# A twelve-layer latent network: keys of the first cross-attention by features, norms in halves, the last layer in one piece

## The reference

```python
def _L0_xattn_ref(x, latents, mask, ...):          # x = ctx_1024, latents = layernorm(x), 16 heads of 64
    xn = layernorm(x, ln_x_g, ln_x_b)
    ln = layernorm(latents, ln_l_g, ln_l_b)
    q = ln @ Wq
    kv = concatenate([xn @ Wkv, ln @ Wkv], axis=1)  # 1601 + 64 keys of each batch
    sim = rmsnorm(q, qn_g) * scale @ rmsnorm(k, kn_g).T
    attn = softmax(where(padded_mask, sim, max_neg))
    return attn @ v @ Wout + bout
...
def _L2_xattn_ref(x1, x2, x3, mask, Wq, Wk, Wv):    # x2 = x3 = ctx_1024, one head of 256
    weights = softmax(q @ k.T / 16 + mask)
    return weights @ v
...
def _L3_ffn_ref(x, W_qkv, b_qkv, W_gate, b_gate, W_experts, b_experts):
    attn_out = softmax(q @ k.T / 4) @ v             # 16 heads of 16, over the 64 latents of a batch
    gate = softmax(x @ W_gate + b_gate)             # 8 experts, the top 2 kept
    expert_out = einsum('bsd,edf->bsef', x, W_experts) + b_experts
    moe_out = einsum('bsef,bse->bsf', expert_out, combine)
    return attn_out + moe_out
...
    x = x + _L0_xattn_ref(ctx_1024, _layernorm(x, axis=-1), ...)   # and eleven more: L0_attn ... L3_ffn
```

## Time and profile before

| | |
|---|---|
| time, median of 3 runs | 3185.78 us (3185.38 to 3188.05) |
| the profiled execution | 3181.54 us, its span 3179.8 us |
| mean granted clock of PE | 0.947 |
| PE busy (matmul) | 2795.1 us, 88% |
| DVE busy | 1643.3 us, 52% |
| ACT busy | 1091.3 us, 34% |
| POOL busy | 522.6 us, 16% |
| L0_xattn | 8.4 to 1254, 1245.6 us |
| L1_xattn, L1_attn, L1_ffn | 504, 295, 223 us |
| L2_xattn, L2_attn, L2_ffn | 137, 95, 167 us |
| L3_xattn, L3_attn, L3_ffn | 234, 53, 117.8 us |

### The profile page before, as it was taken

How to read it: one execution, slowest core, us unless ns; L and a number is a source line. 1 busy time by engine, 2 the same in 40 slices (tenths; PEclk the granted TensorE clock), 3 DMA queues, 4 the chain that set the end, 5 groups by cost and what they waited for, 6 DMA issues and landing times. The chain is left out here.

```text
span 3179.8 us, 43613 instructions
## 1 busy us (share of the span) xinstructions
PE 2795.1 (88%) x17456; PEld 1893.7 (60%) x17456; DVE 1643.3 (52%) x3618; ACT 1091.3 (34%) x1933; POOL 522.6 (16%) x280
## 2 busy tenths in 40 slices
PE   5899999999999998779999978998975689799876
PEld 2466666666666666545656535665962357688644
DVE  5556465655656443545555545763541250177563
ACT  2333333333333332225555436641321252211120
POOL 2112020202112000000000004761010041144200
PEclk8899999999999999889999989998987799899898
DMA  4123223131323211130100000115857338543001
GB/s 141 46 54 67 64 59 78 44 78 45 67 55 67 55 45 34 69 125 22 43 22 22 1 6 34 43 32 187 304 193 250 107 88 301 207 166 124 33 1 33
DMA packets 92096, 271.40 MB, mean 85 GB/s; under 512 B 7920, under 2 KB 57096, under 8 KB 85240
## 3 DMA queue, kind: packets, MB, share of 16 engines
q1 hardware_dynamic: 87896, 259.65, 26.9%
q0 software_dynamic: 2976, 8.13, 0.7%
q10 hardware_dynamic: 1024, 0.86, 0.1%
HBM read 256.64 MB, written 11.44 MB: 84 GB/s over the span
## 5 line engine op out<-in xcount | busy, mean ns | idle before, releaser
L1375 PE MATMUL L_xattn_bank<-L_xattn_keys_tok,L_xattn_probsT 119*128 119x257 f32 (+1 forms) x1792 | 451.5, 392 | 9.2 <-ACT L_xattn_probsT L1211 0.4
L1312 PE MATMUL L_xattn_wide<-L_xattn_keys_feat,weights_a 128*128 128x512 f32 (+2 forms) x1024 | 382.9, 517 | 1.3 <-DVE L_xattn_k_rnorm L1024 0.7
L1375 PEld LDWEIGHTS L_xattn_bank<-L_xattn_keys_tok,L_xattn_probsT 119*128 119x128 f32 (+1 forms) x1792 | 320.0, 190 | 96.1 <-issue 33.1
L1312 PEld LDWEIGHTS L_xattn_wide<-L_xattn_keys_feat,weights_a 128*128 128x128 f32 x1024 | 190.4, 191 | 151.8 <-issue 125.4
L1020 DVE COPY L_xattn_k_normed<-L_xattn_wide 128x833 f32<-128x833 f32 (+1 forms) x128 | 131.3, 1026 | 227.6 <-PE L_xattn_wide L1312 227.6
L2313 DVE TENSOR_TENSOR_SCAN L_attn_state<-L_attn_decay,L_attn_banks 128x1024 f32<-128x1024 f32 x80 | 182.7, 2286 | 69.6 <-PE L_attn_banks L2516 61.6
L1590 DVE CUSTOM_DVE_ANT_0 L_xattn_scores<-L_xattn_banks,L_xattn_mask 128x512 f32<-128x512 f32 (+1 forms) x256 | 131.5, 570 | 151.8 <-issue 151.8
L1126 POOL TENSOR_TENSOR L_xattn_keys_tok<-L_xattn_keys_tok,weights_a 119x1792 f32<-119x1792 f32 (+2 forms) x24 | 61.1, 2547 | 850.3 <-DVE L_xattn_keys_tok L965 850.3
L2419 POOL TENSOR_TENSOR L_attn_state<-L_attn_state,L_attn_C_rows 128x1024 f32<-128x1024 f32 x80 | 188.8, 2362 | 70.1 <-DVE L_attn_state L2313 70.1
L1205 ACT ACTIVATE L_xattn_scores<-L_xattn_scores,L_xattn_neg_max 128x833 f32<-128x833 f32 x128 | 119.6, 982 | 205.9 <-DVE L_xattn_neg_max L1045 205.9
L2516 PEld LDWEIGHTS L_attn_banks<-L_attn_B_diagonal,L_attn_dt_u_tok 128*128 128x128 f32 x1280 | 150.4, 193 | 66.3 <-issue 64.7
(11 more groups left out here) (503 smaller groups left out, 4648.1 us busy)
## 6 DMA issues: line engine op xcount, KB each, us to landing
L_xattn_k_scale<-L_xattn_k_scale_rows SPq DMA_DIRECT2D x128, 417.0 KB, 5.0
L_xattn_ctx_feat<-in_ctx_feat SPq DMA_DIRECT2D x24, 1601.0 KB, 10.7
L_ffn_expert_w<-in_x_L_ffn SPq DMA_DIRECT2D x16, 2056.0 KB, 7.9
L_ffn_expert_w<-in_x_L_ffn SPq DMA_DIRECT2D x15, 1028.0 KB, 6.2
L_ffn_expert_w<-in_x_L_ffn SPq DMA_DIRECT2D x15, 1024.0 KB, 5.9
L_attn_C_rows<-L_attn_c_rows SPq DMA_DIRECT2D x48, 256.0 KB, 3.2
L_xattn_ctx_tok<-in_ctx_tok SPq DMA_DIRECT2D x8, 1536.0 KB
L_xattn_ctx_tok_and_one<-in_ctx_tok SPq DMA_DIRECT2D x8, 1536.0 KB
```

What stands on the lines that cost most here:

```text
L1312: last = nc.tensor.matmul(wide[:, 2 * h + c, 0:n], wk[:, k, p * P:(p + 1) * P], xnT[b % 2][:, k, a:a + n], start=(k == 0), stop=(k == KT - 1))
L1375: last = nc.tensor.matmul(bS[:, 0:D + 1], pT[0:r, c, a, :, :].rearrange("p h q -> p (h q)"), xn[b % 2][0:r, t, :], start=(i == 0), stop=(i ...
```

## The change

1. **Keys by features in L0_xattn.** For batches 1 to 7, `turn_keys` and `keys_turned` are gone. SP loads the context by features at p = 2 (1601 KB). After the last turned weights of the step at p = 3, PE transposes the small table of means and reciprocal deviations (28 x 119, `turn_norms`), DVE copies it out, SP writes it to DRAM and spreads its two rows over all partitions at p = 4. GpSimd then copies the latents' 64 columns, subtracts the row of means and multiplies by the row of reciprocal deviations (four instructions of 128 x 1601, in front of the gains and the mask row of the same batch), and ACT multiplies by and adds the gains at p = 6, two instructions of 128 x 1601. PE's keys at p = 0 wait for these. DVE's `ctx_norm` moves by a step, to p = 3 and 4. Batch 0 keeps its transposes, but its statistics and norm are spread over the loop of the query projection.
2. **Norms in halves**, in all layers: two tiles at a time; epsilon becomes the bias of ACT's Ln (one DVE instruction less); the transposed halves are halves of the tokens; the filler is one matmul of 512 and one of 128 columns.
3. **No block for the weights.** The loads of the next weights are issued in the SP program of the layer that runs: in L1_xattn and L3_xattn behind the loads of batch 0, in L2_xattn behind all its loads, in L0_xattn behind the latents, elsewhere first.
4. **L2_xattn**: four buffers for `ctx_feat`, loads in another order, `scores(u)` in the turn of pair u, with four filler matmuls behind it.
5. **L3_ffn**: `attention_and_experts` takes the place of both functions. The experts' matmuls stand between the pieces of attention; ACT scales an expert's output into SBUF (`ys`), GpSimd adds the eight up (`total`, 128 x 1024 each), and DVE adds the total to x at the end. `experts` is removed.

```diff
-def keep_busy(L, bank, n):
+    for h in range(2):
+        rstd = L.rstd[:, 2 * h:2 * h + 2]
+        act.wait_ge(ln_stats_ready, 2 * nx + h + 1)
+        nc.scalar.activation(rstd, L.mv[:, 2 * h:2 * h + 2, 1], ACT.Ln, bias=L.eps[:, 0:1]).then_inc(rstd_ready, 1)
+        act.wait_ge(rstd_ready, 4 * nx + 2 * h + 1)
+        nc.scalar.activation(rstd, rstd, ACT.Exp, scale=-0.5).then_inc(rstd_ready, 1)
...
+    for h in range(2):
+        if z_ready is not None:
+            pe.wait_ge(z_ready, seen + h + 1)
+        for k in range(KT):
+            for t in (2 * h, 2 * h + 1):
+                c = k * 2 * P + (t % 2) * P
+                last = nc.tensor.transpose(wide[:, h, c:c + P], z[:, t, k * P:(k + 1) * P], L.ident)
+        last.then_inc(zT_turned, 1)
+
```

```diff
+                load_feat(3)
+                load_mask(1)
+                load_tok(2)
+                for u in range(1, PAIRS):
+                    if u + 1 < PAIRS:
+                        load_feat(2 * u + 2)
+                    load_tok(2 * u + 1)
+                    if u + 1 < PAIRS:
+                        load_feat(2 * u + 3)
+                        load_mask(u + 1)
+                        load_tok(2 * u + 2)
...
-                scores(0)
                 for u in range(PAIRS):
-                    if u + 1 < PAIRS:
-                        scores(u + 1)
+                    scores(u)
+                    keep_busy(L, ps[:, 4, :], 4)
                     turn_weights(u)
                     mix(u)
```

```diff
+                def spread_norms(b):
+                    sp.wait_ge(norm_cols_ready, b)
+                    for i in range(2):
+                        sp.dma_start(norm_rows[b % 2, i].rearrange("(t n) -> t n", n=TR), norm_cols[i:2 * TILES:2, :]
+                                     ).then_inc(norm_stored, 16)
+                    sp.wait_ge(norm_stored, 32 * b)
+                    if b >= 2:
+                        sp.wait_ge(feat_scaled, 2 * (b - 1))
+                    for i in range(2):
+                        sp.dma_start(norm_bc[:, i, :], norm_rows[b % 2, i:i + 1, 0:CTX].broadcast_to([P, CTX])
+                                     ).then_inc(norm_moved, 16)
...
+                    if p == 2 and b < B - 1:
+                        load_feat(b + 1)
+                    if p == 4 and b < B - 1:
+                        spread_norms(b + 1)
...
+                    if p in (1, 2):
+                        ctx_stats(0, p - 1)
+                    if p in (3, 4):
+                        ctx_norm(0, p - 3)
...
+                        if p == 3:
                             ctx_norm(b + 1, 0)
-                        if p == 3:
+                        if p == 4:
                             ctx_norm(b + 1, 1)
...
+                def keys_by_feature(b):
+                    pool.wait_ge(feat_loaded[b % 2], 16 * ((b + 1) // 2))
+                    nc.gpsimd.tensor_copy(xnT[b % 2][:, :, CTX:KC], L.zT[:, :, b * S:(b + 1) * S]).then_inc(feat_ready, 1)
+                    pool.wait_ge(norm_moved, 32 * b)
+                    for k in range(KT):
+                        x = xnT[b % 2][:, k, 0:CTX]
+                        nc.gpsimd.tensor_tensor(x, x, norm_bc[:, 0, :], ALU.subtract).then_inc(feat_shifted, 1)
+                    for k in range(KT):
+                        x = xnT[b % 2][:, k, 0:CTX]
+                        pool.wait_ge(feat_shifted, 2 * (b - 1) + k + 1)
+                        nc.gpsimd.tensor_tensor(x, x, norm_bc[:, 1, :], ALU.mult).then_inc(feat_scaled, 1)
...
+                def keys_gained(b, k):
+                    act.wait_ge(feat_scaled, 2 * (b - 1) + k + 1)
+                    x = xnT[b % 2][:, k, 0:CTX]
+                    g, o = at["ln_x_gc"] + k, at["ln_x_bc"] + k
+                    nc.scalar.activation(x, x, ACT.Identity, scale=w[:, g:g + 1], bias=w[:, o:o + 1]
+                                         ).then_inc(feat_ready, 1)
...
+                    elif p == 0:
+                        pe.wait_ge(feat_ready, 3 * b)
...
+                    if g == 3 and p == 3 and b + 1 < B:
+                        turn_norms(b + 1)
+
+                def turn_norms(b):
+                    pe.wait_ge(ctx_rstd_ready, 4 * b + 4)
+                    nc.tensor.transpose(bT[0:2 * TILES, 1, 384:384 + TR], mv[0:TR, :, :].rearrange("p t i -> p (t i)"),
+                                        L.ident[0:TR, 0:TR]).then_inc(norm_turned, 1)
```

```diff
+                dve.wait_ge(x_added, NT)
+                dve.wait_ge(y_added, E)
+                chain(nc.vector.tensor_tensor(L.x[:, :, :], L.x[:, :, :], total[:, :, :], ALU.add))
...
+                def scale_expert(e):
+                    act.wait_ge(y_done, e + 1)
+                    if e == 0:
+                        act.wait_ge(comb_ready, 1)
+                    if e >= 2:
+                        act.wait_ge(y_added, e - 1)
...
+                def expert(e):
+                    pe.wait_ge(experts_loaded[e // 4], 16)
+                    if e >= 2:
+                        pe.wait_ge(y_scaled, e - 1)
...
+                scores(0, 0)
+                scores(0, 1).then_inc(scored, 1)
+                expert(0)
+                pe.wait_ge(s_taken, 2)
+                scores(1, 0)
+                scores(1, 1).then_inc(scored, 1)
+                expert(1)
+                expert(2)
+                pe.wait_ge(s_taken, 4)
+                turn_probs(0)
+                expert(3)
+                turn_probs(1)
+                weigh(0)
+                expert(4)
+                weigh(1)
...
+                expert(6)
+                turn_probs(3)
+                weigh(2)
+                expert(7)
+                weigh(3)
+                project(2)
+                project(3)
```

```diff
         for n, (name, pack, run) in enumerate(packs):
-            if n + 1 < len(packs):
-                with nc.Block() as block:
-                    @block.sync
-                    def _(sp):
-                        load_weights(sp, n + 1)
+            def load_next_weights(sp):
+                if n + 1 < len(packs):
+                    load_weights(sp, n + 1)
+            L.load_next_weights = load_next_weights
```

874 lines of the change are left out of this document (464 added, 410 removed).

## The result

The changed kernel takes 3140.34 us, the median of 4 runs (3130.97 to 3147.97), against 3186.91 before (3185.38 to 3197.05, 4 runs): a ratio of 0.9846, with a 95% interval of 0.9812 to 0.988. It is faster by 1.5%, 47 us, where 96 were forecast, and it lies 10 us above the range. The profiled execution is the slowest of the four, the one of 3147.97, span 3146.2.

| stretch | before | after | difference |
|---|---|---|---|
| ahead of L0_xattn | 8.5 | 7.4 | -1.1 |
| L0_xattn | 1245.5 | 1299.2 | +53.7 |
| L0_attn, L0_ffn | 54.4, 45.8 | 54.7, 45.8 | +0.3 |
| L1_xattn | 504.5 | 491.3 | -13.2 |
| L1_attn, L1_ffn | 294.4, 222.9 | 290.8, 222.9 | -3.6 |

The account below looks back on a forecast made before the run. PE bounds L0_xattn, waits bound L3_ffn. Terms -37.4 + 1.4 + 47.6 - 6 - 7.4 - 10 - 9.6 - 34 - 41 = -96.4 from 3181.54 gave 3085.1; with the median 4.2 above, 3090, range 3058 to 3130.

Parts of the forecast that it names:

- The removed work: L0_xattn, batches 1 to 7: two key transposes of 1.36 us and the 2.63 stall at p = 3 go, -37.4 us.
- The small transpose on PE: L0_xattn: one 28 x 119 transpose per batch behind the turned weights, 0.2 us each, +1.4 us in all.
- The second meeting: L0_xattn: `keys_normed` meets GpSimd's work again at p = 6, after p = 5, costing 3.8 us per batch.
- Rival A: L0_xattn: lock costs 11 us per batch, or a third meeting at p = 7; 30 us more, 3120; chance 0.14.
- the 6.8: L0_xattn: stalls per batch from `keys_normed` meeting GpSimd, 3.0 us at p = 5 plus 3.8 at p = 6; +47.6 in all.
- the lower bound: L0_xattn: at least two stalls of the present kind without remainder, 2 x 2.25 = 4.5 us per batch, 31.5 in all.
- both unknown ends: Ends of the two largest unknowns: the lock in L0_xattn (-16, +30) and the last layers (-15, +19).
- Start of L0_xattn: Batch 0's norm spread over the query projection loop; about half of 11.67 us falls into gaps: -6 (0 to -10).
- L1_xattn: PE's 9.57 us wait for the context's features goes, as the next weights load behind them: -9.6 (-5 at least).
- Blocks and norms: Between and in layers: ten blocks of 0.74 us removed, -7.4; halved norms save 1.0 in each of ten layers, -10.
- L2_xattn: Pairs cost PE 19.0 us; DMA at 338 GB/s takes 87 us and sets the end, 2477 instead of 2511: -34.
- L3_ffn: Filler and the experts' waits of 1.75 us go, stretch 76.7 instead of 117.8: -41 (-31 to -47).

Follow-up runs that it names:

- the best version: Changed kernel with ctx_norm at p = 2 and 3, GpSimd's instructions in short pieces, and two fillers of 512 columns ahead of each norm's transposes: 3050.1 us, ratio 0.9569.

## Why the prediction was wrong

**What has to be explained.** The sum was -96.4 between two profiled executions; they differ by 33.6 us (3147.97 and 3181.54), so 63 are missing. By the stretches 48 of them are in L0_xattn (+53.7 for +5.6), 9 in L2_xattn, and 6 in the other norms and blocks. The median is 50 us over the forecast because the profiled execution is the slowest of its four.

**The removed work was right.** The steps at p = 3 and with transposes are back at 17.2; short pieces, which leave nearly only this term of L0_xattn, give L0_xattn 34 us less than before. The small transpose on PE, forecast at 0.2 us a batch, costs nothing: it takes 0.27 us of PE at p = 4, and that step is 17.24 long like its neighbours.

```profile
762.13 0.27 PE L1824 MATMUL L_xattn_bank<-const,L_xattn_ctx_mean_rstd 119*28 119x119 f32 x1
```

The 0.17 us more stand at p = 1 from the second batch on, in the last batch too, which has no small transpose. There the first mixing of a batch begins 0.2 us later than in other steps; the changed program has two more waits in front of it. That these are the reason is not shown.

**The step that failed: who meets GpSimd.** "`keys_normed` runs 7.97 into a step and so meets GpSimd at p = 5 and at p = 6": the duration was nearly right (3.33 forecast, 3331 ns measured for the multiplication and 3613 for the subtraction), and the list of the instructions that meet GpSimd was too short. It left out `ctx_norm`, although held the hint: 11.67 us for 14 instructions which take 0.41 alone. Two of the 14, beside GpSimd's first gains, took 3.94 and 3.93. The part on the change told that `ctx_norm` moves by a step, and gave that move no price. That is the miss: in the changed kernel the second piece sits at the end of p = 4, beside GpSimd's start, and in six of seven batches four or five of its seven instructions wait 3.1 to 3.8 us each. That makes 94.1 us of stalls for 47.6, and these 46 us are most of the 63. With the norm a step earlier 42.8 are left, all of them at `keys_normed`: that part of the sum held. The Trainium skill has the rule, in the section of "SBUF — State Buffer" that the prediction drew on, Who interferes with whom: `tensor_scalar` can take the shared pair too, in a mode with two ports. The trace agrees that it is shut out (0.41 and 3.64 us); in which mode it ran no run here shows. The prediction used the sentence on two inputs and not the one on modes.

**The second meeting did not come as drawn.** GpSimd's start was forecast 2 us into p = 5 and lay half a microsecond ahead of it (771.69, the step at 772.25). Two microseconds later the seven, 2.35 us when nothing holds them, would have been through. The long step and the first 4 us of the next then held the whole sequence (to 808.2), so there was one step with a meeting in a batch, not two. Rival A (3120) had more stalls, but at p = 7, and is wrong in its mechanism as well. With the norm a step earlier the drawing was close: one long step and 6.1 us a batch for two and 6.8. That this comes so near is in part luck, since the 6.8 has a slip: at p = 6 its own terms (half of 3.7, and 3.2 to 3.7, less 0.9) give 4.2 to 4.7 and not 3.8, so 50 to 54 us in all and not 47.6. The 2.25 of the lower bound is not worked out anywhere either; the present stall is 2.63. The GpSimd instruction of 4.38 us in the earlier trace rows is the addition of the gains (L1128), not a multiplication, which changes no term. And the range adds both unknown ends below (-31) but not above, where both (+49) would have reached 3139.

**Start of L0_xattn.** The first key projection starts at 70.8 instead of 75.2, 3.3 us of it inside the layer, forecast 6.

**L1_xattn.** -13.2 for -9.6 and its share of blocks and norms (1.7): right, and 1.9 us more. The idle of 9.57 is gone, and the first use of the context takes 11.30 us where it took 13.77, which the sum did not have.

**Blocks and norms.** 9.9 us for 15.7 in nine layers. The blocks gave 0.7 each, as forecast. The halves do save, and part of it is given back at the lower clock, since the filler was shortened with them. In L0_ffn nothing was left, and L3_attn is 2.3 us longer than before. The prediction had the filler in its text and no price for it.

**L2_xattn.** -25 for -34. A pair costs PE 19.46 us where nothing waits (2428.47 to 2447.93), 19.0 forecast; but the tokens were waited for twice. PE in L2_xattn of the changed kernel, then its DMA from the start of the layer to 2505, about the end of its transfers:

```profile
2417.65 5.75 PE L1106 MATMUL L_xattn_banks<-z_feat,weights_a 128*128 128x512 f32 x8 [0.83 <-issue]
...
2464.64 8.28 PE L1148 MATMUL L_xattn_banks<-L_xattn_ctx_tok,L_xattn_probsT 128*64 128x256 f32 x52 [4.70 <-DMA L_xattn_ctx_tok<-in_ctx_tok]
...
2490.16 7.47 PE L1148 MATMUL L_xattn_banks<-L_xattn_ctx_tok,L_xattn_probsT 128*64 128x256 f32 x52 [4.21 <-DMA L_xattn_ctx_tok<-in_ctx_tok]
```

```profile
DMA packets 15739, 29.50 MB, mean 318 GB/s; under 512 B 479, under 2 KB 13168, under 8 KB 15735
```

The first line is the lower clock again, 5.75 us for a projection that took 3.67 before. Transfers ran without a break at 318 GB/s for 93 us, where 338 for 87 had been forecast; and they did not only set the end, as the sum had it, but held up the second and third pair (4.70 and 4.21 of idle, and mixings of 8.28 and 7.47 for 5.83). The mis-sized terms are the rate, taken from a stretch of 40 us (5.5 us), and the assumption that PE can make up behind a late transfer: it can't, since a pair costs it 19.4 us whenever it starts. So the layer ended about 18 us behind its last transfer (2523 for 2505) and not 12.5.

**L3_ffn.** -41.7 for -41. In the window above PE is busy for 62.35 of 75.70 us, where the sum had 62.9 of 76.7. No run tests its terms one by one.

**The spread.** The four runs of the changed kernel span 17 us. One meeting more or less makes a long step of 29 or of 32 us, seven times; which one it is may hang on when the transfer of the norm rows lands, since GpSimd starts behind it. The kernel with the norm earlier spans 5.4 us, that with short pieces 5.3; but the one with both spans 11 and the kernel before 12, so chance has a part in it too, and the reading of the spread is argued, not shown.

What stays open: in the profiled execution of the best version L1_attn took 296.6 us where it took 290.8 in all the others with the change; it is the slowest of its five runs, and no run was made for it.

## What to carry to other kernels

Two engines that shut each other out pay by the instruction, not by the microsecond of work: cut the long instructions of the engine off the path (here 3.3 to 3.6 us into pieces of about 1, with the gains cut too, worth 82 us of 3140), before looking for a better place for them. When an edit gives GpSimd work, list every DVE instruction that reads and writes SBUF in those microseconds, the one-input ones and the ones that the same edit moves too, and give each a price. A filler ahead of a layer is part of the layer's time: when it is shortened, look at the first matmuls behind it and their granted clock.

## What the runs showed of the hardware

DVE's scalar subtract and multiply of 119 x 256 from SBUF to SBUF, with one tensor input, takes 0.41 us alone and 3.1 to 3.8 us while GpSimd runs instructions of 3.1 to 3.8 us; from 771.7 to 789.2 us of the changed kernel, where both have some queued, the two engines take turns, one instruction each. With pieces of about 1 us on GpSimd seven of them take 6.02 us, with 1.8 to 2.0 us 9.89, with 3.3 to 3.6 us 18.20. PE's first projection in L3_attn takes 3.69 us behind two fillers of 512 columns (two traces) and 6.37 to 6.64 behind one of 512 and one of 128 (eight traces); in L0_attn it takes 3.69, and 5.08 to 6.53 in seven of the eight.
